# Small and narrow products of a graph-convolution kernel moved to halves of the array's columns, in a new written-out order

## The reference, cut to what matters

```python
x = x + attention(_gn(x))        # linear attention, 4 heads of 32
x = x + graph(_gn(x))

def attention(x):                # per image, N = 1024 tokens
    q, k, v = split(w_qkv @ x)
    q = softmax(q, over the head's 32 channels) * scale
    k = softmax(k, over tokens)
    out = w_out @ ((k @ v.T) applied to q) + b_out
    return norm(out over the whole sample) * gn_weight + gn_bias

def graph(x):
    xn = x / |x|  per token
    sim = xn.T @ xn              # 1024 x 1024
    val, idx = top_k(sim, 9);  v = val / (sum(val) + 1e-6)
    out = silu(group_norm(gather(xn @ w1, idx) weighted by v + b1))
    out = silu(group_norm(gather(out @ w2, idx) weighted by v + b2))
    return out
```

## Time and profile before

| | |
|---|---|
| median of 3 runs | 667.05 us |
| profiled execution | 665.36 us, span 663.6 us |
| PE (products) busy | 631.2 us, 95% of the span, 3958 records |
| PE (weight loads) busy | 321.6 us, 48% |
| DVE busy | 537.4 us, 81% |
| ACT busy | 450.6 us, 68% |
| POOL busy | 498.7 us, 75% |
| mean granted TensorE clock | 0.995 |
| chain that ended last | PE 51%, POOL 13%, DVE 12%, issue 11%, ACT 6%, DMA 5% |
| costliest line | L1120, 232.3 us on PE |

### The profile page before, as it was taken

One profiled execution on the slowest core, in us unless ns is written; L12 is line 12 of the kernel. 1 busy time (PEld: TensorE's weight loads), 2 busy tenths in 40 slices (PEclk: granted clock), 3 DMA queues, 4 the chain that ended last, 5 costly groups with the idle time before them and its releaser, 6 DMA issues.

```text
span 663.6 us, 12573 instructions
## 1 busy us (share of the span) xinstructions
PE 631.2 (95%) x3958; PEld 321.6 (48%) x3958; DVE 537.4 (81%) x1008; ACT 450.6 (68%) x942; POOL 498.7 (75%) x534
## 2 busy tenths in 40 slices
PE   9999999999999999999999999999999999999995
PEld 7676645353544445353545445353535445344452
DVE  3468889898897988898898989898898988868821
ACT  3557577687867777687868678687859777563321
POOL 1225977968897878889888979788888878788810
PEclk9999999999999999999999999999999999989999
DMA  2015445444344445445453544444343544545401
GB/s 66 1 34 112 97 80 105 88 91 76 85 86 96 105 102 98 96 89 89 96 82 80 111 96 97 96 95 83 81 80 69 108 88 89 97 96 97 80 17 33
DMA packets 148723, 55.78 MB, mean 84 GB/s; under 512 B 138008, under 2 KB 138512, under 8 KB 148656
## 3 DMA queue, kind: packets, MB, share of 16 engines
q1 hardware_dynamic: 148656, 54.97, 41.2%
HBM read 12.87 MB, written 4.32 MB: 26 GB/s over the span
## 4 chain that ended last, share of the span: by engine, by line
PE 51%; POOL 13%; DVE 12%; issue 11%; ACT 6%; DMA 5%; SPq 1%; POOLq 0%; DVEq 0%; ACTq 0%
PE pC L1120 23%; PE pS L1083 8%; POOL adj L570 5%; POOL adj L565 3%; PE pB L962 3%; ACT adj L709 2%; PE pA L994 2%; DVE kstat L791 2%; ACT ek L640 2%; DVE top L869 2%; DMA rbc<-rn_row 2%; PE pB L1021 2%; PE pA L1035 2%; PE pA L977 2%; DVE mask L884 2%
## 5 line engine op out<-in xcount | busy, mean ns | idle before, releaser
L1120 PE MATMUL pC<-adj,xt 128*64 128x512 f32 x992 | 232.3, 601 | 0.3 <-POOL adj L576 0.2
L869 DVE MAX8 top<-pS 128x8 f32<-128x1024 f32 x128 | 155.2, 1225 | 23.8 <-ACT adj L709 23.7
L570 POOL TENSOR_TENSOR adj<-maskT,adj 128x128 f32<-128x128 f16 (+3 forms) x127 | 163.5, 1287 | 13.8 <-DMA maskT<-mask 13.7
L884 DVE MATCH_REPLACE8 mask<-top,pS 128x1024 uint16<-128x1024 f32 x128 | 155.2, 1213 | 0.0
L709 ACT COPY adj<-pS 128x1024 f32<-128x1024 f32 x128 | 128.3, 1005 | 27.1 <-PE pS L1085 26.4
L1083 PE MATMUL pS<-xn 64*128 64x512 f32 x256 | 142.0, 642 | 3.0 <-DMA xsw<-xn 1.6
L1083 PE MATMUL pS<-xn,xsw 64*128 64x512 f32 x256 | 141.2, 642 | 0.2
L565 POOL TENSOR_TENSOR adj<-maskT,adj 128x128 f32<-128x128 f16 (+6 forms) x111 | 128.5, 1157 | 0.0
L1120 PEld LDWEIGHTS pC<-adj,xt 128*64 128x64 f32 x992 | 63.5, 136 | 100.1 <-issue 94.5
L576 POOL TENSOR_TENSOR adj<-adj,selves 128x128 f32<-128x128 f32 x127 | 58.5, 461 | 7.1 <-ACT selves L696 0.2
L1085 PEld LDWEIGHTS pS<-mark,place 64*128 64x128 f16 x256 | 24.1, 94 | 72.8 <-issue 72.8
(11 more groups left out here) (151 smaller groups left out, 1074.7 us busy)
## 6 DMA issues: line engine op xcount, KB each, us to landing
xs<-x SPq DMA_DIRECT2D x32, 128.0 KB, 2.8
vbc<-v_row SPq DMA_DIRECT2D x32, 128.0 KB, 3.0
rbc<-rn_row SPq DMA_DIRECT2D x30, 128.0 KB, 2.9
xsw<-xn SPq DMA_DIRECT2D x30, 128.0 KB, 2.3
out<-res SPq DMA_DIRECT2D x30, 128.0 KB, 2.5
maskT<-mask SPq DMA_TRANSPOSE x128, 3.1
cst<-packed SPq DMA_DIRECT2D x1, 471.5 KB, 3.9
y1sw<-y SPq DMA_DIRECT2D x2, 128.0 KB, 2.3
```

Of the source, the lines that this page charges most:

```text
L570: pool.tensor_tensor(above, m[:, r, 0:r + 1, :].bitcast(F16), above, ALU.mult).then_inc(done["upper"], 1)
L869: dve.max(top[b % 2][:, r, 0:TOP], pS[r % 2][:, :]).then_inc(done["tile_top"], 1)
L884: dve.match_replace(out=mask[n % MASKS][:, :], in_to_replace=top[b % 2][:, r, 0:TOP], in_values=pS[r % 2][:, :], imm_value=ONE_BITS).then_ ...
L1120: mm = pe.matmul(ps[h * C:(h + 1) * C, 0:H], xt[:, t % NJ, t // NJ, :], adj[b % 2][:, t, h * H:(h + 1) * H], start=(t == 0), stop=(t == NT ...
```

## The change

1. `average` issues two products, one on each half of the columns (128*64), in place of one of 128*128.
2. `ss`, `xt1` and `xt2` do the same: eight products of 128*64 in place of four of 128*128.
3. The two rows are made by a product with the identity (128*64, two records) and no longer by a transpose (128*8, one record). For this `rn` and `vrec` are widened from 8 to 64 columns, of which the new ones are filled with zeros once; that makes three more fills before the work starts.
4. `rstd` on GpSimd waits for one more semaphore: that the result of the norm of the image before has been used.
5. The order is written anew for all engines. On the tensor engine, in each image, similarity tile 4 comes one aggregation step earlier; the mean `in` comes among aggregation products and not right behind a similarity tile; `m` comes behind the second or third `g2` product and not ahead of the first. On ScalarE the copy of `ky` and the second `silu` change places with copies of similarity tiles; on VectorE the variance of `mi` (L766) comes ahead of the scale and bias of `g2` (L777, L779). On SyncE the loads of `xs` of several images move: before, those of images 10, 13 and 15 were issued just ahead of or among the DMAs of `unit`, and after the change they are not.
6. In `WARM` five entries are resized (three in the first image, two in the last three) and one of the last image is dropped.

```diff
-        rn = sb("rn", [P, NT])
+        rn = sb("rn", [P, C])
...
-        vrec = [sb(f"vrec{i}", [P, NT]) for i in range(2)]
+        vrec = [sb(f"vrec{i}", [P, C]) for i in range(2)]
...
+        NORMED = {"in": "y_ready", "at": "at_normed", "mi": "y1_ready", "g1": "y2_ready", "g2": "y3_ready"}
-        PREPARED = 7
+        PREPARED = 10
...
+            for narrow in (rn, *vrec):
+                pool.memset(narrow[:, :], 0.0).then_inc(done["prepared"], 1)
...
             def rstd(b, tag):
                 pool.wait_ge(*of(f"{tag}_veps", b))
+                pool.wait_ge(*of(NORMED[tag], b - 1))
...
-                pe.matmul(ps[:, 0:n + 2], const(avg), spread_mean[tag][:, :], start=True, stop=True).then_inc(done[f"{tag}_mean_ps"], 1)
+                for c in (slice(0, C), slice(C, P)):
+                    mm = pe.matmul(ps[c, 0:n + 2], const(avg)[:, c], spread_mean[tag][:, :], start=True, stop=True)
+                mm.then_inc(done[f"{tag}_mean_ps"], 1)
...
-                    mm = pe.matmul(pB[:, j:j + NJ + 1:NJ], sq[:, j * P:(j + 1) * P], const("halves"), start=True, stop=True)
+                    for c in range(2):
+                        mm = pe.matmul(pB[c * C:(c + 1) * C, j:j + NJ + 1:NJ], sq[:, j * P + c * C:j * P + (c + 1) * C], const("halves"),
+                                       start=True, stop=True)
...
-                    pe.transpose(pB[0:NT, P:2 * P], rn[:, :], ident).then_inc(done["rn_T"], 1)
+                    pe.matmul(pB[0:C, P:2 * P], rn[:, :], ident, start=True, stop=True).then_inc(done["rn_T"], 1)
...
-                    mm = pe.matmul(pB[:, j * P:(j + 1) * P], xn[b % 2][:, j * P:(j + 1) * P], w1[:, :], start=True, stop=True)
+                    for c in range(2):
+                        mm = pe.matmul(pB[c * C:(c + 1) * C, j * P:(j + 1) * P], xn[b % 2][:, j * P + c * C:j * P + (c + 1) * C], w1[:, :],
+                                       start=True, stop=True)
...
-                pe.transpose(pB[0:NT, 2 * P:3 * P], vrec[b % 2][:, :], ident).then_inc(done["v_T"], 1)
+                pe.matmul(pB[0:C, 2 * P:3 * P], vrec[b % 2][:, :], ident, start=True, stop=True).then_inc(done["v_T"], 1)
...
-                    mm = pe.matmul(pC[:, j * P:(j + 1) * P], y2[:, j * P:(j + 1) * P], w2[:, :], start=True, stop=True)
+                    for c in range(2):
+                        mm = pe.matmul(pC[c * C:(c + 1) * C, j * P:(j + 1) * P], y2[:, j * P + c * C:j * P + (c + 1) * C], w2[:, :],
+                                       start=True, stop=True)
```

More of the change, by code:

```diff
@@ L35 @@
         "attend": [
-            [0], [1], [5], [8], [9], [13], [31], [39], [65], [75], [85], [99], [114], [134], [144], [161]],
+            [0], [1], [2], [3], [7], [11], [33], [46], [62], [68], [97], [99], [114], [129], [144], [166]],
         "unit": [
-            [2, 3, 4], [14, 15, 17], [27, 28, 30], [42, 43, 45], [56, 57, 59], [71, 72, 74], [87, 88, 90], [102, 103, 105],
-            [117, 118, 120], [131, 132, 135], [147, 148, 150], [162, 163, 165], [176, 177, 179], [189, 190, 192],
-            [204, 205, 207], [217, 219, 221]],
+            [4, 5, 6], [14, 15, 17], [27, 28, 30], [41, 42, 44], [56, 57, 59], [72, 73, 75], [86, 87, 89], [102, 103, 105],
+            [117, 118, 120], [132, 133, 135], [147, 148, 150], [161, 162, 164], [176, 177, 179], [189, 190, 192],
+            [203, 204, 206], [218, 219, 221]],
         "neighbours": [
[7 rows of a table removed]
[7 rows of a table added]
         "convolve": [
[3 rows of a table removed]
[3 rows of a table added]
     },
@@ L55 @@
         "attend": [
-            [0, 1], [2, 8], [13, 31], [45, 63], [80, 95], [110, 128], [140, 161], [174, 193], [209, 227], [242, 260],
-            [275, 293], [308, 326], [341, 359], [374, 392], [405, 424], [440, 458]],
+            [0, 1], [2, 8], [15, 31], [48, 63], [77, 95], [109, 128], [143, 161], [176, 193], [209, 226], [242, 260],
+            [275, 293], [308, 326], [341, 359], [374, 392], [407, 424], [440, 458]],
         "unit": [
[4 rows of a table removed]
[4 rows of a table added]
         "weights": [
[16 rows of a table removed]
[16 rows of a table added]
         "convolve": [
[3 rows of a table removed]
[3 rows of a table added]
     },
@@ L224 @@
     ("attend", 0, 1): (24, "pA", "prepared", 1), ("attend", 0, 4): (8, "pB", "yT_copied", 1),
-    ("attend", 0, 5): (24, "pB", "yT_copied", 1), ("attend", 0, 7): (8, "pA", "ekT_copied", 1),
+    ("attend", 0, 5): (25, "pB", "yT_copied", 1), ("attend", 0, 7): (6, "pA", "ekT_copied", 1),
     ("attend", 0, 8): (10, "pB", "m_copied", 1), ("attend", 1, 0): (7, "pA", "qh_copied", 1),
     ("unit", 0, 0): (8, "pA", "qh_copied", 1), ("attend", 1, 1): (13, "pA", "qh_copied", 1),
-    ("unit", 0, 1): (22, "pC", "u_ready", 1), ("unit", 0, 2): (22, "pC", "u_ready", 1),
+    ("unit", 0, 1): (22, "pC", "u_ready", 1), ("unit", 0, 2): (21, "pC", "u_ready", 1),
     ("neighbours", 0, 0): (6, "pA", "q_sub", 2), ("attend", 1, 8): (10, "pB", "xt1_copied", 1),
@@ L233 @@
     ("neighbours", 1, 1): (16, "pA", "q_sub", 3), ("attend", 2, 8): (10, "pB", "xt1_copied", 2),
-    ("neighbours", 1, 3): (4, "pA", "qh_copied", 3), ("unit", 15, 3): (10, "pA", "qh_copied", 16),
-    ("convolve", 13, 10): (4, "pA", "qh_copied", 16), ("neighbours", 15, 3): (9, "pA", "qh_copied", 16),
-    ("convolve", 13, 19): (9, "pA", "qh_copied", 16), ("convolve", 14, 9): (5, "pA", "qh_copied", 16),
-    ("neighbours", 15, 8): (14, "pA", "qh_copied", 16), ("convolve", 14, 10): (16, "pA", "qh_copied", 16),
-    ("convolve", 14, 11): (6, "pA", "qh_copied", 16), ("convolve", 15, 9): (19, "pC", "g2_read", 15),
-    ("convolve", 15, 10): (27, "pA", "g1_read", 16), ("convolve", 15, 11): (6, "pA", "g1_read", 16),
-    ("convolve", 15, 19): (22, "pA", "g1_read", 16),
+    ("neighbours", 1, 3): (4, "pA", "qh_copied", 3), ("convolve", 13, 10): (17, "pA", "qh_copied", 16),
+    ("neighbours", 15, 3): (9, "pA", "qh_copied", 16), ("convolve", 13, 19): (9, "pA", "qh_copied", 16),
+    ("convolve", 14, 9): (5, "pA", "qh_copied", 16), ("neighbours", 15, 8): (14, "pA", "qh_copied", 16),
+    ("convolve", 14, 10): (16, "pA", "qh_copied", 16), ("convolve", 14, 11): (6, "pA", "qh_copied", 16),
+    ("convolve", 15, 9): (20, "pC", "g2_read", 15), ("convolve", 15, 10): (27, "pA", "g1_read", 16),
+    ("convolve", 15, 11): (6, "pA", "g1_read", 16), ("convolve", 15, 19): (22, "pA", "g1_read", 16),
 }
@@ L542, in unit @@
                 pool.wait_ge(*of("ss_read", b, 2))
-                pool.tensor_tensor(rn[:, :], ssq[:, :], minus_half[:, :], ALU.pow).then_inc(done["rn_ready"], 1)
+                pool.tensor_tensor(rn[:, 0:NT], ssq[:, :], minus_half[:, :], ALU.pow).then_inc(done["rn_ready"], 1)
                 yield
@@ L875, in tops @@
                 dve.wait_ge(*of("v_T", b - 2))
-                dve.reciprocal(vrec[b % 2][:, :], vtot[:, :]).then_inc(done["v_rec"], 1)
+                dve.reciprocal(vrec[b % 2][:, 0:NT], vtot[:, :]).then_inc(done["v_rec"], 1)
             def masks(b):
```

2 lines of the change are left out of this document (1 added, 1 removed), and 266 rows, old and new, of the table PLACES.

## The result

The kernel after the change takes 663.12 us (median of 5 runs, 661.82 to 663.83); the kernel before took 667.05 beside it on the same chip (5 runs, 664.59 to 667.47). The ratio is 0.9933, with an interval of 0.9906 to 0.996: 0.7% faster, about 4 us, where 10.5 us were forecast. The profiled execution took 663.12 us, with a span of 661.1; before it was 665.36 with 663.6.

A forecast was written before the change was run, and what follows sets the result against it. PE was taken as nearly full (busy 35.8 of 37.0 us per image), DVE only 4 us behind. Gains 7.2 + 1.3 + 2.0 = 10.5 us gave 654.9 profiled, 656.5 as median; forecast 651 to 661, range 646.5 to 665.

The forecast's parts named there:

- late `xsw`: PE's wait for exchanged unit vectors: moving three `xs` loads out of the row's way gains 1.3 us, ends 0 and 1.6.
- start and end: First two and last two images: cheaper means and `ss` on the path, with resized zero products, gain 2.0 us.
- Stretch A: `vT` to the keys: `mi`, `in` and `at` save 0.71 us, less 0.26 for `mi`'s chain; gain 0.45 per image.
- Stretch B: Keys to `rnT`: faster `ss` worth nothing behind the key exponential; longer `rnT` on the path costs 0.15 us per image.
- Stretch C: Queries to `g2_7`, PE full: `xt1` and `xt2` gain 0.23 us each, `m` costs up to 0.16; gain 0.30 per image.
- The sum: All images: 0.45 + 0.30 - 0.15 - 0.05 = 0.55 us per image, 7.2 us for stretches of 13 images.
- rival 2: New waits (`xt2`'s copy, `ky`'s copy, mask of tile 2) take half, leaving 0.3 us per image: about 661; chance 0.15.
- POOL's added wait: Wait for a norm of the image before, already satisfied, on the chain to `mi`: costs 0.05 us per image.
- full gain: Waits move along because DVE is fed earlier too: 1.25 us per image, about 647; chance 0.13.
- nothing: Every saved switch is taken by a chain: 665.5 to 668 us; chance 0.07.
- Rival 4: Slower at tile 0 and `mi`: late unit vectors leave only costs, 0.36 us per image, 671.7 us; chance 0.06.
- Rival 5: Weights not hidden under the other pair: `xt1` and `xt2` take 1.43 us instead of 0.96, total 668.9; chance 0.02.

The follow-up runs named there:

- rows_back: The kernel after the change, with the two rows made by transposes of 8 columns again: 659.28 us, ratio 0.9879 to the kernel before.
- order_old_products: The kernel before with the new order and resized zero products, but the old products and transposes: 668.99 us, ratio 1.0028.
- xt_only: The kernel before with only `xt1` and `xt2` as eight products on halves of the columns: 669.62 us, ratio 1.0035.
- products_old_order: The kernel after with its new products, but the order and zero products of the kernel before: 665.78 us, ratio 0.9981.
- again: The kernel after the change, unchanged, timed and profiled once more: 662.63 us, ratio 0.992 to the kernel before.
- shift48: The kernel after with 34 zero products at the start instead of 36, plus 24 tiny ones (44 more PE instructions): 664.42 us, ratio 0.9958.
- shift160: The kernel after with 25 zero products at the start instead of 36, plus 80 tiny ones (138 more PE instructions): 668.01 us, ratio 1.0022.
- rows_ss_back: rows_back with the sums of squares as products of 128*128 again, 503 PE instructions per image: 668.22 us, ratio 1.0007 to the kernel before.
- bad_phase: good_phase with 22 more zero products of the first image split in two (44 more instructions, same columns): 671.44 us, ratio 1.0068 to the kernel before.
- good_phase: rows_back with two of four `ss` blocks as 128*128, and zero products of the first image split to place fetches: 658.96 us, ratio 0.9866.
- means_only: The kernel before with only the five means per image as two products on halves of the columns: 667.63 us, ratio 1.0006.

## Why the prediction was wrong, and where it was right

The direction and most of the mechanism on PE held, and 663.12 us lies within the wide range (646.5 to 665), though not in that of the forecast itself (651 to 661). The size did not hold: of 10.5 us, 3.9 came. The step that failed is the late `xsw`, put at a gain of 1.3 us and measured as a cost of 4.5; next to it, start and end gave 0.5 us for 2.0. By its own steps:

1. **Stretch A, 0.45.** The stretch went from 11.12 to 10.68 us in the best images, 0.44, and by 0.38 on the mean of eleven. The 0.26 us taken off because `mi` waits for its chain stands in the trace as 0.22 us of idle. Right.
2. **Stretch B, cost 0.15.** `rnT` 0.36 where 0.35 was forecast, key maximum to `rnT` 5.34 us as before. The faster `ss` was worth nothing, by the wait that had been named. So far right. But the row is not a cost of its own on the path: behind it `xt2` waits for the `silu`, and with the rows as transposes again (rows_back) the gain was nil.
3. **Stretch C, 0.30, against that 0.15.** `rnT` to `vT` went from 20.34 to 20.19, and from 20.48 to 20.33 in images of the other length: 0.15 for a forecast of 0.15. `xt1` and `xt2` 0.97 to 0.98 for 0.96, and `m` costs 0.11 for 0.16 (order_old_products). The sum is right. Its terms don't simply add, by the wait of step 2: `xt2` could gain its full 0.23 only because `rnT` had become longer, since it can't start before the `silu` has ended. In xt_only, where `rnT` is short, `xt1` and `xt2` bring 0.16 to 0.22 together and not 0.46.
4. **The sum, 7.2.** Between the two key maxima 445.54 - 442.51 = 3.0 us were gained, while the lateness in it grew from 1.8 to 5.3. Without it the gain is 6.5 over 12 images, 0.54 per image for a forecast of 0.55. That counts lateness in full. The five images that are undisturbed in both traces gained 0.27 to 0.59, 0.43 on the mean. Nearly right either way, and too much for a new wait like those of rival 2 (0.3 left per image). The price of POOL's added wait was measured by no run.
5. **Late `xsw`, gain 1.3: this step failed.** It cost 3.5 us up to the last key maximum and 1.0 behind it. The reason given, that loads of `xs` stand in the way in most of the waits, holds for one late image of before (`rnT` at 436.7), and that one is indeed undisturbed after. At 362.3 there was a fetch at 7.8; the same image of products_old_order has the same loads of `xs`, no fetch there, and no lateness. At 250.9 there was the packet of `q14`. So there was little to gain, and the step had no term for the other side: a change in PE's instruction count moves every fetch. That put three of them beside `xsw`, 3.7 us, and the slow write at 100.8 brought 1.8. For this last one the cause stays open, as said above.
6. **Start and end, gain 2.0: half failed.** The start gave 96.84 - 95.48 = 1.4. The end lost 1.9, of which 1.0 is the image at 543.7, late by its fetch. The rest, 0.9, goes with the clock. After, from 578 to 585 us TensorE was granted about half its speed, the lower of its two levels of 1.2 and 2.4 GHz (stretch, busy times as above, clock):

```profile
578.00:585.00 7.00, 7.00 (x35) 3.94 (x37) 3.04 (x7) 3.50 (x7) 6.57 (x7) 0.52 0.30 65
```

Such a stretch lasts 6.8 us after and in `again`; 3.4 us in the kernel before, order_old_products, rows_back, shift48, shift160, good_phase and bad_phase; and it is missing in products_old_order, means_only and rows_ss_back. PE had been idle 0.83 us just ahead of the fall in the kernel after, and 1.24 us in the kernel before. What made it twice as long is not settled: the `WARM` entry that the change drops is missing in shift48 and rows_back too, and there the stretch is short, so that entry alone isn't the cause. With the lateness of its two images taken off, the end takes 121.9 and 122.0 us in the two traces with 6.8 us of half clock, 119.7 to 120.5 in the five kernels of the new order and products with 3.4, and 118.8 in rows_ss_back without any. That is about 2 us for the longer stretch, argued from different kernels and not from a run that changes the clock alone.

In the sum of the profiled executions: 6.5 for the images, -3.5 and -1.0 for lateness, 1.4 at the start, -0.9 at the end otherwise, together the 2.5 us of the spans (663.6 - 661.1). The -0.9 is what is left over, so the sum is no check of it.

The rivals: full gain (647) and nothing were not met. Rival 2 came nearest in size, 661, but by its own reason it would have left 0.3 us per image, and 0.43 to 0.54 came. Of its waits (`xt2`'s copy behind the two `silu`, `ky`'s copy, the mask of tile 2) none appeared ahead of `m`, `g2_0` or tile 4; the wait for a `silu` that there is holds up the loads of `xt2`, not its copy, and hides under the longer `rnT`. Rival 4 named the right place, tile 0 and the landing of the unit vectors, and its condition, over 0.3 us late in most images, was not met in the kernel after (5 of 14). It was in shift48, shift160, rows_ss_back and bad_phase (8, 10, 11 and 13), at 664.42 to 671.44 us beside the 671.7 that it gave. That bad_phase comes near it is chance, since the rival's terms were others. Rival 5 is refuted: 16 records of 128*64 take 0.97 us, not 1.43.

The best versions measured have the new order, the new products and the rows as transposes: 658.96 us (good_phase, fetches placed) and 659.28 (rows_back, not placed). Both beat before and after, by their lateness and the shorter half-clock stretch and not by the form of the rows. For good_phase 655 to 657 had been expected; its fetches are out of the way, but in some images (`rnT` at 248.2, 358.8) tile 0 is 0.7 to 1.1 late beside a slower row write or the packets of `q14`. Those were not pursued.

## What to carry to other kernels

When an edit changes how many instructions an engine has, the fetches move against everything periodic, and this kernel, whose chain has a DMA with some 0.3 us of slack, lies 2% apart between a good and a bad placement of them. Compare what an edit does inside undisturbed images first, and then ask of each disturbed one what else was on the DMA queues, and look at all of these queues before one is blamed. Undo a part before you call it a cost: the longer `rnT` looked like 0.15 us per image and was hidden by the wait of a product behind it. A small gain or loss of one part, tried alone, says little on that part: shift the instruction count by some idle instructions and measure it again.

## What the runs showed that was not expected

- A fetch of 16 KB, of which one comes per some 257 of PE's instructions, made the transfer `xsw` of 128 KB land later: 4.3 for 2.5 us in the pair above, and tile 0 late by over 0.3 us in 40 of 41 images with a fetch 7.6 to 9.5 us after `rnT`.
- 44 instructions without work, in the first of 16 images, changed the time by 12.5 us of 659.
- Small products on two halves of the columns load their weights side by side: 16 loads of 64 columns in `ss` stand in 8 pairs over 0.55 us. The Trainium skill (TensorE: Matmul & The Clock Gate, Part 3, "What overlaps and what doesn't") lets weight loads overlap with running products only where the row group differs. All these products use all 128 rows, and the loads run beside them (the products are the 0.63 us from 318.91 on shown above), so this trace differs from it, as it did before the change:

```profile
318.91 0.55 PEld L1060 LDWEIGHTS pB<-cst,sq 128*64 128x64 f32 x16
```
